# 2304 instead of 2048 of a tile's 4096 attention columns turned by DMA, with the mask loads of a tile issued in a row

## What is computed

```python
q = x @ Wq.T + bq
k = x @ Wk.T + bk
v = x @ Wv.T + bv
scores = q @ k.T / sqrt(128)
scores = where(adj > 0, scores, -9e15)
attention = softmax(scores, axis=-1)
y = x + elu(attention @ v)
out = (y - mean(y)) / sqrt(var(y) + 1e-5)
```

## Time and profile before

| | |
|---|---|
| median of three runs | 428.9 us |
| profiled execution | 429.13 us |
| its span | 427.3 us |
| busy of the span: PE / DVE / ACT / POOL | 97% / 84% / 83% / 83% |
| granted TensorE clock, mean | 0.998 |
| data moved by DMA | 104.8 MB, 245 GB/s |

### The profile page before, as it was taken

One profiled execution on the slowest core, in us unless ns is written; L12 is line 12 of the kernel. 1 busy time (PEld: TensorE's weight loads), 2 busy tenths in 40 slices (PEclk: granted clock), 3 DMA queues, 4 the chain that ended last, 5 costly groups with the idle time before them and its releaser, 6 DMA issues.

```text
span 427.3 us, 11462 instructions
## 1 busy us (share of the span) xinstructions
PE 416.2 (97%) x3470; PEld 311.3 (73%) x3470; DVE 360.8 (84%) x677; ACT 353.8 (83%) x742; POOL 354.0 (83%) x644
## 2 busy tenths in 40 slices
PE   7997999999999999999999999999999999999994
PEld 6764777767777777777777777777777777777784
DVE  3889988888888898888888988888889888888784
ACT  4987788888888889888888898888888988888892
POOL 0596578988898889888988898889888988898875
PEclk9999999999999999999999999999999999999999
DMA  8944999899999999999999999999999999998550
GB/s 253 399 161 111 266 275 251 208 294 263 286 268 254 275 264 267 238 280 266 259 251 280 268 265 244 272 271 263 245 277 271 256 250 271 263 267 225 104 103 21
DMA packets 149794, 104.77 MB, mean 245 GB/s; under 512 B 132755, under 2 KB 141461, under 8 KB 141717
## 3 DMA queue, kind: packets, MB, share of 16 engines
q1 hardware_dynamic: 149344, 104.41, 92.0%
q10 hardware_dynamic: 436, 0.20, 0.2%
HBM read 69.47 MB, written 2.10 MB: 167 GB/s over the span
## 4 chain that ended last, share of the span: by engine, by line
POOL 58%; issue 18%; PE 10%; DMA 4%; ACT 3%; DVE 2%; POOLq 2%; SPq 2%; ACTq 0%; DVEq 0%
POOL p_rows L409 26%; POOL res L423 5%; POOL var_eps L445 4%; POOL rstd L447 4%; POOL att_sum L416 3%; POOL y L428 3%; POOL neg_mean L434 3%; POOL att L418 3%; POOL centred L436 2%; POOL expm L425 2%; DMA p_turned<-p_rows 2%; PE ps_out L967 2%; POOL y_out L451 2%; DMA x_rows<-in_x_dram 2%; POOL var L443 1%
## 5 line engine op out<-in xcount | busy, mean ns | idle before, releaser
L409 POOL TENSOR_TENSOR p_rows<-scores,p_rows 128x256 f16<-128x256 f32 x252 | 177.0, 733 | 7.3 <-ACT p_rows L566 7.1
L696 DVE CUSTOM_DVE_ANT_0 scores<-ps_scores,adj 128x1024 f32<-128x1024 f32 x128 | 155.9, 1218 | 13.0 <-issue 9.3
L549 ACT ACTIVATE scores<-scores,neg_max 128x1024 f32<-128x1024 f32 x128 | 145.8, 1139 | 3.5 <-DVE neg_max L706 3.5
L712 DVE TENSOR_TENSOR p_lo<-ps_t,p_hi 128x512 f16<-128x512 f32 x124 | 82.6, 686 | 28.4 <-ACT p_hi L558 28.3
L682 DVE TENSOR_SCALAR adj<-adj 128x1024 f32<-128x1024 int32 x128 | 103.5, 810 | 0.2
L928 PE MATMUL ps_scores<-k_hi,q_hi 128*128 128x512 f16 x256 | 97.0, 379 | 0.5 <-DVE max_parts L696 0.5
L929 PE MATMUL ps_scores<-k_lo,q_hi 128*128 128x512 f16 x256 | 97.0, 379 | 0.0
L930 PE MATMUL ps_scores<-k_hi,q_lo 128*128 128x512 f16 x256 | 97.0, 379 | 0.0
L967 PE MATMUL ps_out<-v_parts,p_turned 128*128 128x256 f16 x496 | 95.0, 273 | 0.4 <-DMA p_turned<-p_rows 0.3
L967 PE MATMUL ps_out<-v_parts,p_hi 128*128 128x256 f16 x496 | 95.1, 273 | 0.0
L969 PE MATMUL ps_out<-v_parts,p_lo 128*128 128x128 f16 x496 | 88.5, 219 | 0.0
(11 more groups left out here) (121 smaller groups left out, 479.8 us busy)
## 6 DMA issues: line engine op xcount, KB each, us to landing
adj<-in_adj_dram SPq DMA_DIRECT2D x63, 1024.0 KB, 5.3
out_dram<-y_out SPq DMA_DIRECT2D x32, 64.0 KB, 4.9
x_rows<-in_x_dram SPq DMA_DIRECT2D x4, 256.0 KB, 4.4
x_rows<-in_x_dram SPq DMA_DIRECT2D x2, 512.0 KB, 7.6
adj<-in_adj_dram SPq DMA_DIRECT2D x2, 512.0 KB, 7.4
p_turned<-p_rows SPq DMA_TRANSPOSE x63, 4.5
w_rows<-in_L_gnn_Wq_dram ACTq DMA_DIRECT2D x1, 64.0 KB, 2.7
w_rows<-in_L_gnn_Wk_dram ACTq DMA_DIRECT2D x1, 64.0 KB, 3.3
```

Of the source, the lines that this page charges most:

```text
L409: last = nc.gpsimd.tensor_tensor(p_rows[c][:, w:][:, cols], s_sb[s][:, c * PIECE:c * PIECE + w][:, cols], p_rows[c][:, 0:w][:, cols], ALU. ...
L549: nc.scalar.activation(s_sb[s][:, cols], s_sb[s][:, cols], ACT.Exp, bias=neg_max[:, s:s + 1], accum_out=p_sums[:, s, c:c + 1]).then_inc(ex ...
L696: nc.vector.tensor_tensor_reduce(out=s_sb[s][:, cols], in0=ps_scores[c % 2][:, :], in1=mask_sb[s][:, cols], scale=SCALE, scalar=-3.0e38, o ...
L712: nc.vector.tensor_tensor(p_lo[:, k, :], ps_t[bank_of(s, g)][:, :], p_hi[:, k, :], ALU.subtract).then_inc(plo_ready, 1)
```

## The change

Part 1 of the columns that DMA turns grows from 1024 to 1280, by the first 256 columns of group 4 (`MIXED`). So group 4 is transposed by PE in its two upper blocks only, and ACT's high part and DVE's low part of it have 256 columns. Its two lower blocks come out of the turned part 1: ACT writes their high rows (`high_rows_odd`, step 6, after the third exponential), DVE their low rows (`low_rows_odd`, step 7, after the row maximum), and SP's turn of part 1, now 128 x 2560, waits for these as well as for POOL's low rows. POOL's work is the same.

PE's value matmuls keep their number; their order is group 4's upper half, 0, 5, then 1 and 6 in one step, 7, 2, 3, and group 4's lower half (`TURNED_HALF`) in step 7. Part 1's turn is therefore wanted in step 5, before in step 6. ACT makes the high rows of part 1 in step 4, before in step 6.

SP issues both halves of tile p+1 in a row, after part 1's turn and before the store and part 0's turn; before, one half came after each turn. Masks are made one piece later: pieces 1, 2 and 3 of tile p in its own steps 1, 3 and 5, and piece 0 of the next tile in step 7.

The diff, without the renaming of counts (`STEPS` to `PV_PARTS` in waits on `pv_done`):

```diff
-DMA_COLS = (PIECE, PIECE)
+MIXED_COLS = 256
+DMA_COLS = (PIECE, PIECE + MIXED_COLS)
+MIXED = FIRST_PE
-PV_ORDER = (4, 0, 5, 6, 1, 7, 2, 3)
+TURNED_HALF = STEPS
+PV_STEPS = ((4,), (0,), (5,), (1, 6), (7,), (2,), (3,), (TURNED_HALF,))
...
+        def by_pe(g):
+
+            return slice(MIXED_COLS, BANK) if g == MIXED else slice(0, BANK)
...
                 sp.wait_ge(rows_lo, BY_DMA * i + c + 1)
                 sp.sem_inc(turn_begun, 1)
+                if c == 1:
+                    sp.wait_ge(rows_lo_odd, i + 1)
+                    sp.sem_inc(turn_begun, 1)
                 sp.dma_start_transpose(p_turned[c][s][:, :, :], p_rows[c][:, :]).then_inc(turned[c], 16)
...
                 if turns_1:
                     turn(p - 2, n, 1)
-                if head:
+                if loads:
+                    load_half(p + 1, 1 - n, 0, False)
                     load_half(p + 1, 1 - n, 1, False)
                 if stores:
                     store(p - 4, n)
                 if turns_0:
                     turn(p - 1, 1 - n, 0)
-                if loads:
-                    load_half(p + 2, n, 0, False)
...
-                nc.scalar.activation(p_hi[:, k, :], ps_t[bank_of(s, g)][:, :], ACT.Copy).then_inc(phi_ready, 1)
+                nc.scalar.activation(p_hi[:, k, by_pe(g)], ps_t[bank_of(s, g)][:, by_pe(g)],
+                                     ACT.Copy).then_inc(phi_ready, 1)
...
+            def high_rows_odd(i, s, first):
+
+                act.wait_ge(exp_done, exp_count(i, 2))
+                if not first:
+                    act.wait_ge(turned[1], 16 * i)
+                nc.scalar.activation(p_rows[1][:, PIECE:PIECE + MIXED_COLS], s_sb[s][:, 2 * PIECE:2 * PIECE + MIXED_COLS],
+                                     ACT.Copy).then_inc(rows_hi_odd, 1)
...
-                    if j == (3 if not warm and p == 1 else 6) and has_1:
+                    if j == (3 if not warm and p == 1 else 4) and has_1:
                         high_rows(p - 1, 1 - n, 1, not warm and p == 1)
+                    if j == (5 if not warm and p == 1 else 6) and has_1:
+                        high_rows_odd(p - 1, 1 - n, not warm and p == 1)
...
-                nc.vector.tensor_tensor(p_lo[:, k, :], ps_t[bank_of(s, g)][:, :], p_hi[:, k, :],
+                nc.vector.tensor_tensor(p_lo[:, k, by_pe(g)], ps_t[bank_of(s, g)][:, by_pe(g)], p_hi[:, k, by_pe(g)],
                                         ALU.subtract).then_inc(plo_ready, 1)
+
+            def low_rows_odd(i, s):
+
+                w = DMA_COLS[1]
+                dve.wait_ge(rows_hi_odd, i + 1)
+                nc.vector.tensor_tensor(p_rows[1][:, w + PIECE:2 * w], s_sb[s][:, 2 * PIECE:2 * PIECE + MIXED_COLS],
+                                        p_rows[1][:, PIECE:w], ALU.subtract).then_inc(rows_lo_odd, 1)
...
                     if j == 7 and has_scores:
                         row_max(p, n)
+                    if j == 7 and has_1:
+                        low_rows_odd(p - 1, 1 - n)
...
-                        if j == 1:
-                            mask_piece(p, n, 3)
-                        if j in (3, 5, 7) and makes_mask:
-                            mask_piece(p + 1, 1 - n, j // 2 - 1)
+                        if j in (1, 3, 5):
+                            mask_piece(p, n, j // 2 + 1)
+                        if j == 7 and makes_mask:
+                            mask_piece(p + 1, 1 - n, 0)
...
-                for b in range(BLOCKS):
+                for b in range(by_pe(g).start // P, BLOCKS):
                     kb = g * BLOCKS + b
                     last = nc.tensor.transpose(ps_t[bank][:, b * P:(b + 1) * P], s_sb[s][:, kb * P:(kb + 1) * P], ident[:, :])
...
+                g = MIXED if part == TURNED_HALF else part
+                by_dma = part < FIRST_PE or part == TURNED_HALF
+                c = min(g // 2, BY_DMA - 1)
+                if not by_dma:
                     pe.wait_ge(plo_ready, PE_GROUPS * i + g - FIRST_PE + 1)
-                elif g % 2 == 0 or pv_count(0, g - 1) > pv_count(0, g):
-                    pe.wait_ge(turned[g // 2], 16 * i + 16)
+                elif part in (0, 2):
+                    pe.wait_ge(turned[c], 16 * i + 16)
...
-                    if has_2:
-                        values(p - 2, n, PV_ORDER[j], first)
+                    for part in PV_STEPS[j]:
+                        if has_2:
+                            values(p - 2, n, part, first)
```

More of the change, by code:

```diff
@@ L24 @@
 PE_GROUPS = STEPS - FIRST_PE
+MIXED = FIRST_PE
 T_AT = {4: 6, 5: 7, 6: 8, 7: 10}
-PV_ORDER = (4, 0, 5, 6, 1, 7, 2, 3)
+TURNED_HALF = STEPS
+PV_STEPS = ((4,), (0,), (5,), (1, 6), (7,), (2,), (3,), (TURNED_HALF,))
+PV_ORDER = tuple(g for step in PV_STEPS for g in step)
+PV_PARTS = len(PV_ORDER)
 Q_AT = (4, 6, 7, 8, 10, 11, 12)
@@ L173, in attention_kernel @@
         rows_lo = sem("rows_lo")
+        rows_hi_odd = sem("rows_hi_odd")
+        rows_lo_odd = sem("rows_lo_odd")
         turned = [sem(f"turned{c}") for c in range(BY_DMA)]
@@ L313, in turn, with period @@
                 sp.sem_inc(turn_begun, 1)
+                if c == 1:
+                    sp.wait_ge(rows_lo_odd, i + 1)
+                    sp.sem_inc(turn_begun, 1)
                 sp.dma_start_transpose(p_turned[c][s][:, :, :], p_rows[c][:, :]).then_inc(turned[c], 16)
-            def period(p, n, head=True, turns_0=True, turns_1=True, stores=True, loads=True):
+            def period(p, n, turns_0=True, turns_1=True, stores=True, loads=True):
                 if turns_1:
                     turn(p - 2, n, 1)
-                if head:
+                if loads:
+                    load_half(p + 1, 1 - n, 0, False)
                     load_half(p + 1, 1 - n, 1, False)
@@ L338, in _ @@
             sp.dma_start(bv_rows[:, :], bv.rearrange("(a d) -> a d", a=1).to_broadcast([P, D])).then_inc(bv_in, 16)
-            period(0, 0, head=False, turns_0=False, turns_1=False, stores=False)
             period(1, 1, turns_1=False, stores=False)
@@ L345, in _ @@
                     period(2 * pair + n, n)
-            period(TILES - 2, 0, loads=False)
-            period(TILES - 1, 1, head=False, loads=False)
+            period(TILES - 2, 0)
+            period(TILES - 1, 1, loads=False)
             turn(LAST - 1, 0, 1)
@@ L565, in high_rows @@
                     act.wait_ge(turned[c], 16 * i)
-                nc.scalar.activation(p_rows[c][:, 0:w], s_sb[s][:, c * PIECE:c * PIECE + w], ACT.Copy).then_inc(rows_hi, 1)
+                nc.scalar.activation(p_rows[c][:, 0:PIECE], s_sb[s][:, c * PIECE:(c + 1) * PIECE], ACT.Copy).then_inc(rows_hi, 1)
+            def high_rows_odd(i, s, first):
[4 more added lines that the diff above has]
+                                     ACT.Copy).then_inc(rows_hi_odd, 1)
             def attention(i, s):
                 act.wait_ge(recip_ready, i + 1)
-                act.wait_ge(pv_done, STEPS * (i + 1))
+                act.wait_ge(pv_done, PV_PARTS * (i + 1))
                 nc.scalar.activation(att2[:, s, :], ps_out[s][:, 0:2 * D], ACT.Copy, scale=recip[:, s:s + 1]).then_inc(att_ready, 1)
@@ L593, in last_high_part @@
                 act.wait_ge(last_pt, g - LAST_PE + 1)
-                act.wait_ge(pv_done, STEPS * LAST)
+                act.wait_ge(pv_done, PV_PARTS * LAST)
                 nc.scalar.activation(last_high(g), last_ps[g], ACT.Copy).then_inc(last_hi_act, 1)
@@ L789, in period @@
                             mask_piece(0, 0, c)
-                        for c in ((), (), (0,), (1, 2))[j // 2] if j % 2 == 1 else ():
-                            mask_piece(1, 1, c)
+                        if j == 7:
+                            mask_piece(1, 1, 0)
                     elif has_scores:
-                        if j == 1:
-                            mask_piece(p, n, 3)
-                        if j in (3, 5, 7) and makes_mask:
-                            mask_piece(p + 1, 1 - n, j // 2 - 1)
+                        if j in (1, 3, 5):
+                            mask_piece(p, n, j // 2 + 1)
+                        if j == 7 and makes_mask:
+                            mask_piece(p + 1, 1 - n, 0)
                     if j in rows_at:
@@ L945, in transposes, with values @@
                 last.then_inc(pt_ready, 1)
-            def values(i, s, g, first):
-                if g >= FIRST_PE:
+            def values(i, s, part, first):
+                g = MIXED if part == TURNED_HALF else part
+                by_dma = part < FIRST_PE or part == TURNED_HALF
+                c = min(g // 2, BY_DMA - 1)
+                if not by_dma:
                     pe.wait_ge(plo_ready, PE_GROUPS * i + g - FIRST_PE + 1)
-                elif g % 2 == 0 or pv_count(0, g - 1) > pv_count(0, g):
-                    pe.wait_ge(turned[g // 2], 16 * i + 16)
-                if g == PV_ORDER[0] and not first:
+                elif part in (0, 2):
+                    pe.wait_ge(turned[c], 16 * i + 16)
+                if part == PV_ORDER[0] and not first:
```

(20 more changed lines are left out.)

9 lines of the change are left out of this document (4 added, 5 removed).

## The result

The changed kernel takes 445.7 us (median of four runs, 445.06 to 446.44), the kernel before 428.8 us beside it: 1.0398 times the time, with a 95% interval of 1.0384 to 1.0412. I had said slower by 35 us; it is slower by 17. The sign is right, and the time lies in the range, but only because the range reached down to the 433 us of rival A, which is not what happened. The size is off by a factor of two, and that needs a cause.

The account below looks back on a forecast made before the run. PE bounds the kernel before, with SP's DMA queue close behind; after the change the queue decides. 429.1 us + 32 (29 periods at 1.1) + 2 for a DMA pause + 0.5 for the tail = 464 us, range 433 to 482.

Parts of the forecast that it names:

- rival A: First load behind part 1's turn starts warm: period 12.3 us, 433 us; chance 0.12, including times up to the forecast.
- Rival B: Part 0's turn lands by 14.05 us into the period, PE runs at 11.99 us: 422.4 us; chance 0.13.
- B's sum of a period's DMA work: DMA engines' work per period, 6.0 + 2.6 + 2.3 = 10.9 us, said to fit under PE's 11.99.
- T to part 1's issue: From a period's first score matmul on PE to SP's issue of part 1's turn: 1.6 us, bounds 1.25 and 1.9.
- Its landing: Part 1's turn, 20 blocks instead of 16, from issue to landing: 5.2 us, bounds 4.9 and 5.7.
- The rest, load, load, store and turn: SP's queue from part 1's landing to part 0's: 6.0 us for one load and turn, 2.6 for the second load.
- The added operations: Extra pieces for 256 columns: ACT +0.13 us a period (bounds 0, 0.6), DVE +0.15 (bounds 0, 0.7), hidden in idle time.
- my sign of being right: PE's value matmuls wait for the turned part once a period, about 1.3 us each, 30 to 40 us in all.
- whether the stall would loosen itself: It would not: part 1's turn waits for the row maximum, that for the last scores, which come after the stall.
- pause: DMA pause near 76 us, absorbed by slack before the change: 2 us added, bounds 0 and 4.
- tail: End of the run, part 1 of tile 30 landing about 0.9 us later: 0.5 us added, bounds 0 and 1.
- a falling clock: Stalls cool PE's clock in every period, its 12.0 us tending to 24: up to 348 us more; chance 0.02.

Follow-up runs that it names:

- e2: Changed kernel with PE's value matmuls of part 0's first group moved from step 1 to step 2: 436.1 us, ratio 1.0160.
- e1: Changed kernel with DVE's low rows of the 256 columns made before the last masked piece instead of after the row maximum: 440.2 us, ratio 1.0275.
- e7: Changed kernel with the second load of each tile cut from 2048 to 1024 columns from tile 2 on: 427.5 us, ratio 0.9971.
- e8: Changed kernel with a third load of 512 columns (256 KB) between second load and store in periods 2 to 30: 452.3 us, ratio 1.0554.

## Why the prediction was right and wrong

**Right: what decides.** Part 0's turn queues behind two loads, and PE waits for it in step 1. I had said that it would land 7.5 to 8.5 us after issue, with its issue over 4 us, and part 1 near 5.2. From 120 to 410 us the measured values are 7.5 to 8.5, 5.3 to 6.3 and 4.8 to 5.0. e2 moves the time by moving the use of part 0, e1, e7 and e8 by moving its landing. Rival B, that the turn would land in time, was out, and rival A, the warm load, too. The way from part 1's landing to part 0's took 8.5 to 9.4 us in the three periods followed here, where A had 5.0 + 2.6 = 7.6, and behind part 1's turn the first load starts as in the earlier trace rows:

```profile
212.50:213.00 0.50, 0.50 (x5) 0.26 (x4) 0.50 (x1) 0.50 (x2) 0.50 (x2) 1.00 0.51 164
```

For B I had counted part 1's turn with 2.3 us of work for the DMA, its way to landing less 2.9 of start. Here I was wrong: the trace has less start and more work. The turn of part 1 issued at 66.7 us meets an empty queue and lands 4.8 us later:

```profile
66.70:67.80 1.10, 1.10 (x11) 0.75 (x10) 1.10 (x3) 1.10 (x3) 1.01 (x2) 1.00 0.00 0
67.80:71.20 3.40, 3.40 (x33) 2.69 (x32) 3.37 (x8) 3.40 (x9) 2.98 (x6) 1.00 1.15 219
```

Its packets begin 1.1 us after the issue and move for some 3.3 us (the last 0.2 us of the second window hold the next load's first packets too). B's sum of a period's DMA work is then 6.0 + 2.6 + 3.3 = 11.9 us and not 10.9, so B had less for it than I thought. For the same reason the next turn can begin to move at T'+2.7 and not at T'+3.6; that is still after T'+2.07.

**The terms.** T to part 1's issue: 1.6 forecast, 1.75 and 1.79 found. Its landing: 5.2 forecast, 4.8 to 4.9 found, less than in proportion to its 20 blocks. The rest, load, load, store and turn: 8.6 forecast, 8.5 to 9.4 found. Together 15.4; the trace has 15.4, 15.2 and 16.1 in these three periods, and 15.46 in the mean from 116 us on. The added operations had been bounded well; both lie in the trace as one row each:

```profile
L741 DVE TENSOR_TENSOR p_rows<-scores,p_rows x31: 411/418/427, 41.0 to 424.6; 128x256 f16<-128x256 f32 x31
...
L585 ACT ACTIVATE p_rows<-scores x31: 399/401/452, 35.6 to 420.5; 128x256 f16<-128x256 f32 x31
```

0.42 us for DVE's, exactly the estimate, and 0.40 for ACT's where I had 0.36.

**Wrong: the step from the sum to the period.** I wrote "The period is 15.4 - 2.07 = 13.3 us, and PE stands still for 1.3 us in each." The two halves of the sentence exclude each other. If PE stands still for s in each period, the period is 11.99 + s, and part 0 is used at T'+2.07+s, not at T'+2.07. So 11.99 + s + 2.07 + s = 15.4, s = 0.67, and the period is 12.66. I had counted the stall once where it stands twice: in the period's length before T' and in the wait behind it. With the same terms the sum becomes 29 x (12.66 - 12.21) = 13 us, plus the 2.5 for pause and tail: 445 us. Measured: 445.7. That the two agree to within 1 us is in part luck, since the sum leaves out 1.7 us that the clock cost in the profiled run. Rival A's price has the same error in it. So has my sign of being right, a wait of 1.3 us once a period and 30 to 40 us in all: the matmuls wait 18.0 us in 19 places. I had even asked whether the stall would loosen itself, and said no because part 1's turn waits for scores that come after the stall. That is true of the next turn and not of the one under way, which went out at T+1.75, before the stall at T+2.07.

In the trace the 1.3 us that two periods share falls mostly on every second one, because the loop ties each stall to the last but one and leaves two independent chains: 208.11 to 233.27 is one round of the first (25.16), 221.27 to 247.39 of the second (26.12).

The three kernels with this stall can be set beside both ways of counting. For each, the landing of part 0 after T is the mean over the periods from the ninth on (116 to 411 us in the changed kernel). The two-period loop gives half of the sum of that landing and 9.94, the one-period loop the landing less 2.07.

| | landing after T | two-period loop | one-period loop | mean period measured |
|---|---|---|---|---|
| changed kernel | 15.46 | 12.70 | 13.39 | 12.80 |
| e1_odd_early | 15.02 | 12.48 | 12.95 | 12.50 |
| e8_extra_load | 15.83 | 12.88 | 13.76 | 12.90 |

Of the 12.80 the one stretch at the lower clock, told of below, makes 0.07. The two-period loop gives all three within 0.03 us of what is left; the one-period loop is 0.45 to 0.86 too long.

**Other items.** DMA's pause: 2 us forecast. In this profile two periods between 51 and 91 us, 13.5 and 14.1 long, are in line with it; what they cost apart from the loop was not measured. One of 15.8, later, is in part the clock's, below, which my corrected sum doesn't hold. The mean of the 29 periods from the third on is 12.87 us here and 12.28 before, and 29 times the difference is 17 us. The rest is small: the third period starts 0.5 us earlier, and the tail is 1.0 us longer, where I had 0.5.

## What to carry to other kernels

When a late transfer makes an engine wait, draw the loop that closes through that wait and count how many periods it spans: a delay added to a loop of two periods costs half of itself in each. Write the stall as an unknown on both sides before subtracting. And ask of each transfer what stands ahead of it in its queue when it is issued, not how busy the queue is: here the same traffic cost 17 us in one order of use and gained 0.2% in another, by wanting the late part one step later, making DVE's low rows earlier and taking the mask out of DVE's way.

## What the runs showed of the hardware that I had not expected

In the changed kernel's profile, one period is 15.8 us long. A stall of 1.96 us, ending at 247.39, is followed by a stretch at the lower of TensorE's two levels. Here are the stalled matmul and the windows after it (granted clock in the third column from the right):

```profile
247.39 0.28 PE L1003 MATMUL ps_out<-v_parts,p_turned 128*128 128x256 f16 x1 [1.96 <-DMA p_turned<-p_rows]
...
247.40:248.10 0.70, 0.70 (x9) 0.65 (x10) 0.67 (x5) 0.70 (x1) 0.46 (x1) 1.00 1.11 211
248.10:251.50 3.40, 3.40 (x18) 2.36 (x17) 1.07 (x3) 1.37 (x3) 2.67 (x4) 0.50 0.99 200
...
251.50:254.00 2.50, 2.50 (x24) 1.78 (x22) 1.81 (x4) 2.47 (x7) 1.29 (x3) 1.00 0.98 383
```

0.50 is 1.2 GHz. The clock was still full for 0.7 us after PE had resumed, then low for 3.4 us. What it cost can be read from the period: 15.79 less PE's 11.99 and less 2.12, by which the matmul came later than T+2.07, leaves 1.7 us. I had given a falling clock 0.02 and taken it as all or nothing; it came once in the periods of this profiled run. The mean granted clocks of the four runs are 0.994 (the profiled one), 0.992, 0.998 and 0.999, so it may have come in a second of them. The Trainium skill, page "TensorE: Matmul & The Clock Gate", section "HAM oscillation — how this bites in real kernels", describes a clock that falls at waits for DMA; this row agrees that it can. But the length of the wait alone does not say when: in e8_extra_load a stall of 1.98 us, ending at 95.74, left the clock at 1.00 (second window above), and so did the other stalls of the changed kernel, the longest of them 1.91 us at 81.02. What sets it is open.
